# Paired powers on GpSimd, an x ring of fourteen tiles and newly drawn orders in a four-layer graph network

## Chip, cores and metric

The kernel runs on one core of a Trainium2 chip. The metric is the device time in microseconds (us) of one execution. Engines are named as the profile names them: PE (TensorE), DVE (VectorE), ACT (ScalarE), POOL (GpSimd) and SP (SyncE, which issues the loads and stores here).

## What is computed

Thirty-two graphs g, each with 256 nodes of 128 features, pass four pre-norm residual layers. Layers 0 and 3 are graph attention, layer 1 attends with scores of h against itself, and layer 2 is a relational convolution with a bias.

```python
h = jnp.maximum(_layernorm(x, axis=-1), 0.0)
x = x + _L0_gnn_ref(h, adj, L0_gnn_W, L0_gnn_a)
h = jnp.maximum(_layernorm(x, axis=-1), 0.0)
x = x + _L1_gnn_ref(h, adj, L1_gnn_a0, L1_gnn_a1, L1_gnn_a2, L1_gnn_a3)
h = jnp.maximum(_layernorm(x, axis=-1), 0.0)
x = x + _L2_gnn_ref(h, L2_gnn_adj, adj, L2_gnn_weight, L2_gnn_bias)
h = jnp.maximum(_layernorm(x, axis=-1), 0.0)
x = x + _L3_gnn_ref(h, adj, L3_gnn_W, L3_gnn_a)      # _L3 ends in elu
...
def _layernorm(x, axis=-1, eps=1e-05):
    return (x - m) / jnp.sqrt(v + eps)
```

## The kernel before

A unit is one layer of one graph. `ORDER` lists all 128 units: layer 0 of graphs 0 to 15, then layers 1, 2 and 3 of the same sixteen, and then the same four stages for graphs 16 to 31. So there are two halves of four stages of sixteen units. Unit n is number n of this list: 48 to 63 are the first layer 3, 64 to 79 the second layer 0.

Each engine has one instruction stream, built by `pipeline`. It takes a list of (stage function, lag, layers). At step s it calls each stage of the list, in the list's order, for unit s - lag, if that unit's layer is in layers. So the lag says how many steps a stage runs behind the newest unit, and the list's order says what comes first inside a step. Engines meet only at semaphores: a stage waits until the count of the unit that it needs is reached, and everything behind it on its engine waits too.

What a unit passes through, with its lag before:

- DVE `statistics` (0) and `mean_and_variance` (1) give mean and variance of each node (tile mv, two values per partition).
- POOL `inverse_deviation` (0) raises the variance to the power -1/2: one tensor_tensor with pow per unit, on 128x2 values (rs<-mv, L356).
- In layers 0, 1 and 3, POOL `subtract_mean` (0) and `scale_deviation` (1) make h from x: L365, then L373 in place. In layer 2 the DVE's `minus_mean` and the ACT's `normalize` do it, and POOL `add_bias` (2, xb<-x, L384) adds the bias to x in a ring of eight tiles. For the last eight graphs of a half it waits until `residual` (DVE, L708) of the unit eight before has freed its tile.
- PE `put_hT` (3) transposes h (L863), then come `put_edgesT`, `put_v` (L905), `put_z` (L929 in layer 2, 4 or 5 or 6 by layer) and `put_o` (8; L972 in layer 2, L984 and L987 in layers 0 and 3). ACT takes the products out of PSUM, and masks the edges (`mask_edges`, L493, layer 0).
- DVE `residual` (10) writes the new x. In layer 3 ACT's `elu_parts` (9), DVE's `elu` (12) and `add_x` (13, odd graphs) or POOL's `add_x_even` (10, even graphs, L394) make the result.

h has a ring of twelve tiles, and `put_hT` is given only one PSUM bank (bank 0). The x of layer 0 lies in a ring of `XS` = 12 tiles: the first twelve are loaded at the start, and `load_x` on SP reloads a tile after `residual` of layer 0 has read it. SP's list is load_x (lag 10), load_edges (10) and store (11), so in the turn between the halves a load can stand behind a store in SP's stream.

Of the kernel before, what the change touches and what calls it, by code (L numbers as in the profile page):

```python
# [88 lines left out]
def gat_stack(nc, x, adj, w0, a0, m0, m1, m2, m3, w2, b2, w3, a3, out):  # L89
# [10 lines left out]
    with ctx:  # L100
# [233 lines left out]
        def _(pool):  # L334
# [61 lines left out]
            pipeline([(add_x_even, 10, LAST), (inverse_deviation, 0, MULTI_REL), (add_bias, 2, RGCN_REL),  # L396
                      (inverse_deviation, 0, LAST), (scale_deviation, 1, LAST),
                      (scale_deviation, 1, FIRST), (inverse_deviation, 0, RGCN_REL),
                      (scale_deviation, 1, MULTI_REL), (inverse_deviation, 0, FIRST),
                      (subtract_mean, 0, FIRST), (subtract_mean, 0, LAST), (subtract_mean, 0, MULTI_REL)])  # L400
# [3 lines left out]
            with pool.If(pool.value_load(flag[0:1, 0:1], min_val=0, max_val=P) > 0):  # L404
                with pool.Fori(0, B) as g:
                    for layer in range(4):
# [5 lines left out]
                        pool.tensor_tensor(grs[:, :], gve[:, :], minus_half[:, :], ALU.pow).then_inc(g_step, 1)  # L412

        @block.scalar
        def _(act):
# [143 lines left out]
            pipeline([(scale_v, 6, LAST), (take_hT, 4, LAST), (normalize, 5, RGCN_REL),  # L559
                      (mask_edges, 5, FIRST), (scale_hT, 5, MULTI_REL), (take_edgesT, 6, FIRST),  # L560
                      (exponentials_of_s, 5, FIRST), (upper_part, 6, MULTI_REL), (scale_v, 6, FIRST),
                      (exponentials, 7, MULTI_REL), (take_hT, 4, MULTI_REL), (take_hT, 4, FIRST),
                      (exponentials_of_s, 5, LAST), (take_pT, 8, MULTI_REL), (take_mh, 6, RGCN_REL),
                      (elu_parts, 9, LAST)])
# [525 lines left out]
```

## Time and profile before

| what | value |
|---|---|
| median of 3 runs | 291.73 us (291.55 to 292.25) |
| profiled execution | 291.89 us |
| its span, first to last instruction | 290.1 us |
| PE busy | 275.5 us, 95% |
| ACT busy | 259.7 us, 90% |
| DVE busy | 251.4 us, 87% |
| POOL busy | 235.6 us, 81% |
| mean granted TensorE clock | 0.995 |

The profiled execution spends 1.8 us outside of its span. A share of busy time is an average over eight stages with different limits, so what an engine's time is worth has to be read stage by stage. The chain of work that ended last lies 63% on PE, 10% on POOL, 9% on DVE and 8% on ACT.

### The profile page before, as it was taken

The numbers are of one execution on the slowest core, as the hardware profiler recorded it, in microseconds if no ns is written. First come the engines' busy times: TensorE is split into PE (matmuls) and PEld (weight loads), VectorE is DVE, ScalarE is ACT, GpSimd is POOL, SyncE is SP. The second block draws the span as 40 slices with busy tenths as digits, with TensorE's granted clock in tenths as the row PEclk, the third lists the DMA queues.
The fourth block names the chain that finished last, engine by engine and source line by source line (L and its number), as shares of the span: only waits on it lengthen the run. The fifth ranks groups of instructions, "written<-read, shape, count | busy, mean of one in ns | idle before, by whom it ended". The sixth has DMA issues, their size and how long they took to land.

```text
span 290.1 us, 8093 instructions
## 1 busy us (share of the span) xinstructions
PE 275.5 (95%) x2250; PEld 257.0 (89%) x2250; DVE 251.4 (87%) x1217; ACT 259.7 (90%) x850; POOL 235.6 (81%) x376
## 2 busy tenths in 40 slices
PE   2899999999999999999998999999999999999992
PEld 1799998898899999999978899988899999999991
DVE  4788999988888888999988899988878988799985
ACT  4799998999997888898999899899999788889984
POOL 4799876886658999999999988786765799999922
PEclk9999999999999999999999999999999999999998
DMA  5935555500000000011111470000000000001123
GB/s 183 340 105 164 166 166 163 163 5 0 2 1 2 0 2 3 2 54 58 54 49 47 163 239 2 3 0 2 1 2 1 1 2 0 2 5 55 57 71 113
DMA packets 15949, 17.77 MB, mean 61 GB/s; under 512 B 2720, under 2 KB 11808, under 8 KB 15904
## 3 DMA queue, kind: packets, MB, share of 16 engines
q1 hardware_dynamic: 15488, 17.18, 18.6%
q8 instruction: 19, 0.31, 0.4%
q14 instruction: 26, 0.21, 0.2%
q10 hardware_dynamic: 416, 0.07, 0.1%
HBM read 13.05 MB, written 4.19 MB: 59 GB/s over the span
## 4 chain that ended last, share of the span: by engine, by line
PE 63%; POOL 10%; DVE 9%; ACT 8%; issue 7%; DMA 1%; SPq 0%; DVEq 0%; POOLq 0%; ACTq 0%
PE bank L987 20%; PE bank L934 10%; PE bank L929 6%; PE bank L905 5%; PE bank L863 5%; PE bank L954 5%; POOL h L365 3%; DVE pT L688 3%; PE bank L984 3%; PE bank L972 3%; POOL rs L356 3%; PE bank L942 2%; PE bank L936 2%; POOL h L373 2%; ACT relu_y L556 2%
## 5 line engine op out<-in xcount | busy, mean ns | idle before, releaser
L356 POOL TENSOR_TENSOR rs<-mv,minus_half 128x2 f32<-128x2 f32 x128 | 91.5, 715 | 37.8 <-DVE mv L624 36.3
L987 PE MATMUL bank<-val,pT 128*128 128x129 f32 x512 | 74.6, 275 | 0.0
L987 PEld LDWEIGHTS bank<-val,pT 128*128 128x128 f32 x512 | 67.8, 193 | 0.0
L688 DVE SCALAR_TENSOR_TENSOR pT<-bank,val,edgesT 128x256 f32<-128x256 f32 x128 | 55.6, 476 | 5.9 <-ACT edgesT L503 3.1
L373 POOL TENSOR_TENSOR h<-h,rs 128x256 f32<-128x256 f32 x93 | 57.8, 621 | 1.8
L613 DVE BATCH_NORM_STATS2 st<-x 128x6 f32<-128x128 f32 x192 | 45.6, 279 | 0.0
L905 PE MATMUL bank<-w_gat,hT 128*128 128x131 f32 x256 | 41.0, 284 | 2.8 <-ACT hT L484 2.8
L516 ACT ACTIVATE val<-bank,val 128x128 f32<-128x128 f32 x128 | 41.8, 397 | 0.1
L365 POOL TENSOR_TENSOR h<-x,mv 128x256 f32<-128x256 f32 x64 | 41.3, 645 | 0.2
L863 PE MATMUL bank<-ident,h 128*128 128x128 f32 x192 | 38.0, 280 | 1.0 <-POOL h L373 0.7
L905 PEld LDWEIGHTS bank<-w_gat,hT 128*128 128x128 f32 x256 | 34.4, 194 | 4.8 <-ACT val L516 3.5
L624 DVE BATCH_NORM_AGGREGATE mv<-st 128x2 f32<-128x9 f32 x256 | 32.9, 171 | 5.0 <-DVE st L613 0.5
L934 PE MATMUL bank<-hT,haT 128*128 128x256 f32 x128 | 36.7, 382 | 0.0
L984 PE MATMUL bank<-ident,vsum 128*128 128x128 f32 x128 | 35.5, 277 | 0.6 <-DVE x L714 0.3
L987 PEld LDWEIGHTS bank<-h,pT 128*128 128x128 f32 x256 | 31.3, 191 | 2.9
L987 PE MATMUL bank<-h,pT 128*128 128x129 f32 x256 | 33.8, 275 | 0.0
L929 PE MATMUL bank<-edgesT,h 128*128 128x256 f32 x128 | 32.9, 380 | 0.0
L484 ACT ACTIVATE hT<-bank 128x256 f32<-128x256 f32 x64 | 26.9, 421 | 3.5 <-PE bank L863 3.1
L539 ACT ACTIVATE prob<-neg_s,neg_max 128x256 f32<-128x256 f32 x64 | 29.2, 512 | 0.4 <-DVE neg_max L672 0.4
L463 ACT ACTIVATE h<-x,nb,rs 128x128 f32<-128x128 f32 x64 | 27.9, 486 | 0.0
L555 ACT ACTIVATE expy<-bank,rinv 128x128 f32<-128x128 f32 x64 | 25.2, 398 | 2.5 <-DVE rinv L700 2.3
L863 PEld LDWEIGHTS bank<-ident,h 128*128 128x128 f32 x192 | 24.9, 151 | 1.9 <-issue 1.0
(85 smaller groups left out, 651.5 us busy)
## 6 DMA issues: line engine op xcount, KB each, us to landing
edges<-in_adj SPq DMA_DIRECT2D x32, 256.0 KB, 3.3
xin<-in_x SPq DMA_DIRECT2D x32, 128.0 KB, 2.4
out_x<-result SPq DMA_DIRECT2D x32, 128.0 KB, 1.7
w_rel<-in_L_gnn_weight SPq DMA_DIRECT2D x1, 256.0 KB, 3.2
w_gat<-in_L_gnn_W ACTq DMA_DIRECT2D x1, 64.0 KB, 2.7
w_gat<-in_L_gnn_W SPq DMA_DIRECT2D x1, 64.0 KB, 3.2
a_rel<-in_L_gnn_a SPq DMA_DIRECT2D x4, 0.5 KB, 3.8
bias<-in_L_gnn_bias SPq DMA_DIRECT2D x1, 64.0 KB, 3.4
```

Source lines behind the costliest of these rows:

```text
L356: pool.tensor_tensor(rs[:, g % WIDE], mv[:, g % WIDE, :, 1], minus_half[:, :], ALU.pow).then_inc(rs_ready, 1)
L365: pool.tensor_tensor(h[:, n % HS, :, 0:D], xin[:, g % XS] if layer == 0 else x1[:, g % WIDE], mv[:, g % WIDE, :, 0:1].to_broadcast([P, T, ...
L373: pool.tensor_tensor(h[:, n % HS, :, 0:D], h[:, n % HS, :, 0:D], rs[:, g % WIDE, :].rearrange("p (t o) -> p t o", o=1).to_broadcast([P, T, ...
L516: last = act.activation(val[:, k, t, 0:D], bank_v(n)[:, t, 0:D], ACT.Copy, scale=val[:, k, t, D:D + 1])
L613: last = dve.bn_stats(st[:, g % WIDE, t, 0:6], src[:, t])
L688: last = dve.scalar_tensor_tensor(pT[:, n % 4, u], bank_z(n)[:, 0], val[:, k, u, D + 2:D + 3], edgesT[:, g % WIDE, u], ALU.max, ALU.mult)
L863: last = pe.transpose(bank_x(n)[:, t * P:(t + 1) * P], h[:, n % HS, t, 0:D], ident[:, :])
L905: last = pe.matmul(bank_v(n)[:, t], hT[:, n % 4, t * P:(t + 1) * P], w_gat[layer // 3][:, 0:D + 3], start=True, stop=True)
L929: last = pe.matmul(z[:, 0], h[:, n % HS, u, 0:D], edgesT[:, g % WIDE, u], start=(u == 0), stop=(u == T - 1))
L934: pe.matmul(z[:, t], haT[:, n % 4, t * P:(t + 1) * P], hT[:, n % 4], start=True, stop=False, skip_group_check=True)
L984: pe.matmul(bank_o(n)[:, t, 0:D], vsum[:, k:k + 1].to_broadcast([P, P]), ident[:, :], start=True, stop=False, is_transpose=True, skip_grou ...
L987: last = pe.matmul(bank_o(n)[:, t], pT[:, n % 4, u, t * P:(t + 1) * P], values[:, u], start=(u == 0 and layer == 1), stop=(u == T - 1), sk ...
```

## The change

Three things change. First, POOL's power instruction: units 0 to 3 keep one each, and from unit 4 on the odd unit of each pair does both in one instruction on 128x4 values, so the even unit waits for the odd one's variance. The tile of exponents is widened for that. Second, the x ring has fourteen tiles instead of twelve, so two more loads are issued at the start and the second half has two fewer to wait for a freed tile. Third, the lists of all engines are redrawn: most lags outside of POOL grow by one together. Relative to the others, `put_z` of layer 2 (6 to 5), `mask_edges`, `take_edgesT`, `normalize`, `scale_hT`, `upper_part` and `take_mh` (unchanged) come one or two steps earlier; on POOL `subtract_mean` goes from lag 0 to 2 and `scale_deviation` from 1 to 2, `add_bias` from 2 to 0.

```diff
+PAIRED = 4
-XS = 12
+XS = 14
-LAG_MAX = 13
-SP_LAG = 10
+LAG_MAX = 14
+SP_LAG = 11
...
-        minus_half = sb("minus_half", [P, T])
+        minus_half = sb("minus_half", [P, 2, T])
...
-                if ORDER[n] == (1, 0):
+                if ORDER[n] == (1, 1):
...
                 pool.wait_ge(mv_ready, nth(ALL, n))
-                pool.tensor_tensor(rs[:, g % WIDE], mv[:, g % WIDE, :, 1], minus_half[:, :], ALU.pow).then_inc(rs_ready, 1)
+                if n < PAIRED:
+                    pool.tensor_tensor(rs[:, (g % WIDE)], mv[:, (g % WIDE), :, 1], minus_half[:, 0], ALU.pow).then_inc(rs_ready, 1)
+                elif n % 2 == 1:
+                    i = (g % WIDE) - 1
+                    pool.tensor_tensor(rs[:, i:i + 2], mv[:, i:i + 2, :, 1], minus_half[:, :, :], ALU.pow).then_inc(rs_ready, 2)
...
-            pipeline([(add_x_even, 10, LAST), (inverse_deviation, 0, MULTI_REL), (add_bias, 2, RGCN_REL),
...
+            pipeline([(subtract_mean, 2, LAST), (add_x_even, 12, LAST), (subtract_mean, 2, MULTI_REL),
...
-                      (minus_mean, 2, RGCN_REL),
+                      (minus_mean, 5, RGCN_REL),
```

POOL's stream at the turn from layer 2 to layer 3, before. xb is the bias added to x, rs the power, L365 the subtraction of unit 48 and L373 its scaling; the last xb is that of unit 47.

```order
L384 TENSOR_TENSOR xb<-x,bias_less 128x256
L356 TENSOR_TENSOR rs<-mv,minus_half 128x2
L365 TENSOR_TENSOR h<-x,mv 128x2x128
L384 TENSOR_TENSOR xb<-x,bias_less 128x256
L356 TENSOR_TENSOR rs<-mv,minus_half 128x2
L373 TENSOR_TENSOR h<-h,rs 128x2x128
L365 TENSOR_TENSOR h<-x,mv 128x2x128
L356 TENSOR_TENSOR rs<-mv,minus_half 128x2
L373 TENSOR_TENSOR h<-h,rs 128x2x128
```

The same place after the change (line numbers are six or so higher; L361 is the paired power, L370 the subtraction, L378 the scaling).

```order
L361 TENSOR_TENSOR rs<-mv,minus_half 128x4
L389 TENSOR_TENSOR xb<-x,bias_less 128x256
L361 TENSOR_TENSOR rs<-mv,minus_half 128x4
L370 TENSOR_TENSOR h<-x,mv 128x2x128
L378 TENSOR_TENSOR h<-h,rs 128x2x128
L370 TENSOR_TENSOR h<-x,mv 128x2x128
L361 TENSOR_TENSOR rs<-mv,minus_half 128x4
L378 TENSOR_TENSOR h<-h,rs 128x2x128
L370 TENSOR_TENSOR h<-x,mv 128x2x128
```

What moved: before, the power and the subtraction of unit 48 stood ahead of the last xb. Now both stand behind it, and in an odd unit the next pair's power stands between subtraction and scaling.

PE's stream at the same place, before: L929 is `put_z` and L972 `put_o` of layer 2, L863 the transposes of units 48, 49 and 50, L905 `put_v` of unit 48.

```order
L929 MATMUL bank2<-edgesT,h 128x256 x2
L972 MATMUL bank6<-w_rel,mhT 128x128 x2
L929 MATMUL bank3<-edgesT,h 128x256 x2
L972 MATMUL bank7<-w_rel,mhT 128x128 x2
L863 MATMUL bank0<-ident,h 128x128 x2
L929 MATMUL bank2<-edgesT,h 128x256 x2
L972 MATMUL bank6<-w_rel,mhT 128x128 x2
L863 MATMUL bank0<-ident,h 128x128 x2
L905 MATMUL bank5<-w_gat3,hT 128x131 x2
L929 MATMUL bank3<-edgesT,h 128x256 x2
L972 MATMUL bank7<-w_rel,mhT 128x128 x2
L863 MATMUL bank0<-ident,h 128x128 x2
```

And after the change (L935, L978, L869 and L911 are the same four).

```order
L935 MATMUL bank2<-edgesT,h 128x256 x2
L978 MATMUL bank7<-w_rel,mhT 128x128 x2
L935 MATMUL bank3<-edgesT,h 128x256 x2
L978 MATMUL bank6<-w_rel,mhT 128x128 x2
L935 MATMUL bank2<-edgesT,h 128x256 x2
L978 MATMUL bank7<-w_rel,mhT 128x128 x2
L869 MATMUL bank0<-ident,h 128x128 x2
L935 MATMUL bank3<-edgesT,h 128x256 x2
L978 MATMUL bank6<-w_rel,mhT 128x128 x2
L869 MATMUL bank0<-ident,h 128x128 x2
L911 MATMUL bank5<-w_gat3,hT 128x131 x2
L978 MATMUL bank7<-w_rel,mhT 128x128 x2
```

What moved: two z blocks followed the first transpose before, and one does now. The other has gone to the turn from layer 1 to layer 2, so unit 50's transpose comes closer behind unit 49's.

## Rows read from the trace of the kernel before

**Rows 1.** The page of the profile: span and busy time of each engine.
```profile
span 290.1 us, 8093 instructions
PE 275.5 (95%) x2250; PEld 257.0 (89%) x2250; DVE 251.4 (87%) x1217; ACT 259.7 (90%) x850; POOL 235.6 (81%) x376
```

**Rows 2.** Windows inside the layer-1 stage and the turn from layer 3 to layer 0.
```profile
core 0: us, PE busy (x) PEld busy (x) DVE busy (x) ACT busy (x) POOL busy (x), PEclk, DMA share, GB/s
60.00:80.00 20.00, 20.00 (x152) 17.70 (x151) 16.45 (x96) 19.57 (x48) 14.06 (x24) 1.00 0.00 1
142.00:158.00 16.00, 14.55 (x129) 12.74 (x128) 13.57 (x57) 16.00 (x61) 15.29 (x23) 1.00 0.12 43
```

**Rows 3.** Timeline of TensorE, both layer-3 stages; what ended a wait is in brackets.
```profile
130.85 0.38 PE L863 MATMUL bank<-ident,h 128*128 128x128 f32 x2
133.50 0.41 PE L863 MATMUL bank<-ident,h 128*128 128x128 f32 x2 [0.32 <-POOL h L373]
...
265.32 0.38 PE L863 MATMUL bank<-ident,h 128*128 128x128 f32 x2
267.49 0.38 PE L863 MATMUL bank<-ident,h 128*128 128x128 f32 x2
269.49 0.38 PE L863 MATMUL bank<-ident,h 128*128 128x128 f32 x2
272.16 0.41 PE L863 MATMUL bank<-ident,h 128*128 128x128 f32 x2 [0.33 <-POOL h L373]
```

**Rows 4.** Timeline of GpSimd in the second layer-3 stage.
```profile
265.01 0.90 POOL L394 TENSOR_TENSOR result<-expy,x 128x256 f32<-128x256 f32 x1
269.84 0.90 POOL L394 TENSOR_TENSOR result<-expy,x 128x256 f32<-128x256 f32 x1
```

**Rows 5.** Groups by line and form: GpSimd (columns: busy us, mean ns, idle before).
```profile
L356 POOL TENSOR_TENSOR rs<-mv,minus_half 128x2 f32<-128x2 f32 x128 | 91.5, 715 | 37.8 <-DVE mv L624 36.3 <-PE bank L987 1.1
L341 POOL MEMSET minus_half<- 128x2 f32 x1 | 0.1, 100 | 0.0
```

**Rows 6.** Timeline of the turn from layer 2 to layer 3, second half.
```profile
241.08 0.73 POOL L384 TENSOR_TENSOR xb<-x,bias_less 128x256 f32<-128x256 f32 x1
241.75 0.41 DVE L708 TENSOR_TENSOR x<-bank,xb 128x256 f32<-128x256 f32 x1
241.76 0.70 POOL L356 TENSOR_TENSOR rs<-mv,minus_half 128x2 f32<-128x2 f32 x1
...
246.48 0.38 PE L863 MATMUL bank<-ident,h 128*128 128x128 f32 x2
...
248.01 0.38 PE L863 MATMUL bank<-ident,h 128*128 128x128 f32 x2
249.98 0.38 PE L863 MATMUL bank<-ident,h 128*128 128x128 f32 x2
251.49 0.38 PE L863 MATMUL bank<-ident,h 128*128 128x128 f32 x2
```

**Rows 7.** Timeline of GpSimd at the start: subtract, then its dependent multiply.
```profile
10.00 0.62 POOL L365 TENSOR_TENSOR h<-xin,mv 128x256 f32<-128x256 f32 x1
10.69 0.61 POOL L373 TENSOR_TENSOR h<-h,rs 128x256 f32<-128x256 f32 x1
```

**Rows 8.** Chain that ended last, layer 2: one z block of PE (start, us).
```profile
102.76 0.87 PE bank L929 x4
```

**Rows 9.** Timeline around the late x tile of the second layer-0 stage.
```profile
163.87 0.43 SPq L303 DMA_DIRECT2D xin<-in_x  x1
164.77 0.38 PE L863 MATMUL bank<-ident,h 128*128 128x128 f32 x2
166.10 0.49 DVE L613 BATCH_NORM_STATS2 st<-xin 128x6 f32<-128x128 f32 x2 [0.48 <-DMA xin<-in_x]
167.15 0.68 ACT L493 ACTIVATE absent<-edges 128x512 bf16<-128x512 uint32 x1 [1.11 <-DMA edges<-in_adj]
167.70 0.41 PE L863 MATMUL bank<-ident,h 128*128 128x128 f32 x2
```

More of the change, by code:

```diff
@@ L340, in _ @@
                                    pattern=[[-1, P]], channel_multiplier=1).then_inc(ident_ready, 1)
-            pool.memset(minus_half[:, :], -0.5).then_inc(ident_ready, 1)
+            pool.memset(minus_half[:, :, :], -0.5).then_inc(ident_ready, 1)
             pool.memset(ones[:, :], 1.0).then_inc(ident_ready, 1)
@@ L394, in add_x_even @@
                     pool.tensor_tensor(result[:, k], expy[:, n % 4], x1[:, g % WIDE], ALU.add).then_inc(result_ready[0], 1)
-            pipeline([(add_x_even, 10, LAST), (inverse_deviation, 0, MULTI_REL), (add_bias, 2, RGCN_REL),
[L397 to L400, printed above, removed]
+            pipeline([(subtract_mean, 2, LAST), (add_x_even, 12, LAST), (subtract_mean, 2, MULTI_REL),
+                      (scale_deviation, 2, MULTI_REL), (inverse_deviation, 0, LAST),
+                      (inverse_deviation, 0, MULTI_REL), (scale_deviation, 2, LAST),
+                      (inverse_deviation, 0, RGCN_REL), (add_bias, 0, RGCN_REL), (subtract_mean, 2, FIRST),
+                      (scale_deviation, 2, FIRST), (inverse_deviation, 0, FIRST)])
             pool.wait_ge(flag_ready, 1)
@@ L557, in elu_parts @@
                 last.then_inc(y_ready, 1)
[L559 to L564, printed above, removed]
+            pipeline([(scale_v, 7, LAST), (take_hT, 5, FIRST), (take_hT, 5, MULTI_REL),
+                      (exponentials, 8, MULTI_REL), (take_hT, 5, LAST), (take_pT, 9, MULTI_REL),
+                      (normalize, 5, RGCN_REL), (exponentials_of_s, 6, LAST),
+                      (exponentials_of_s, 6, FIRST), (scale_hT, 5, MULTI_REL), (upper_part, 6, MULTI_REL),
+                      (scale_v, 7, FIRST), (elu_parts, 10, LAST), (take_mh, 6, RGCN_REL),
+                      (mask_edges, 5, FIRST), (take_edgesT, 6, FIRST)])
             act.wait_ge(flag_ready, 1)
@@ L731, in add_x @@
                     dve.tensor_tensor(result[:, k], expy[:, n % 4], x1[:, g % WIDE], ALU.add).then_inc(result_ready[1], 1)
-            pipeline([(invert_sums, 10, LAST), (mean_and_variance, 1, RGCN_REL), (elu, 12, LAST),
-                      (invert_sums, 10, FIRST), (mean_and_variance, 1, LAST), (take_rows, 7, FIRST),
-                      (take_z, 7, MULTI_REL), (statistics, 0, MULTI_REL), (minus_mean, 2, RGCN_REL),
-                      (residual, 10, RGCN_REL), (residual, 10, FIRST), (mean_and_variance, 1, FIRST),
-                      (add_x, 13, LAST), (center_early, 2, FIRST), (statistics, 0, RGCN_REL),
-                      (mean_and_variance, 1, MULTI_REL), (invert_sums, 10, MULTI_REL),
-                      (statistics, 0, LAST), (take_rows, 7, LAST), (rectify, 3, MULTI_REL),
-                      (statistics, 0, FIRST), (residual, 10, MULTI_REL)])
+            pipeline([(statistics, 0, RGCN_REL), (invert_sums, 11, LAST), (invert_sums, 11, FIRST),
+                      (elu, 13, LAST), (statistics, 0, MULTI_REL), (add_x, 14, LAST),
+                      (residual, 11, FIRST), (take_z, 8, MULTI_REL), (mean_and_variance, 1, LAST),
+                      (minus_mean, 5, RGCN_REL), (residual, 11, RGCN_REL),
+                      (mean_and_variance, 1, RGCN_REL), (statistics, 0, LAST),
+                      (invert_sums, 11, MULTI_REL), (take_rows, 8, FIRST),
+                      (mean_and_variance, 1, MULTI_REL), (rectify, 4, MULTI_REL), (take_rows, 8, LAST),
+                      (mean_and_variance, 1, FIRST), (residual, 11, MULTI_REL), (center_early, 2, FIRST),
+                      (statistics, 0, FIRST)])
             dve.wait_ge(scores_taken, COUNTS[MULTI_REL][-1])
```

10 lines of the change are left out of this document (5 added, 5 removed).

## Prediction

> **What bounds the kernel now.** I read the page first. PE is busy 275.5 of 290.1 us, and no other engine is over 90% [rows 1]. Then I read windows by stage. In 60 to 80 us, the layer-1 stage, PE is busy 20.00 of 20 while POOL has 14.06 [rows 2]. Nothing that POOL saves there can show, and the same holds wherever PE's transposes follow each other at their even pace. So I looked on PE's timeline for transposes that come late, and for what ended the wait.
>
> There are three such places. In layer 3 PE runs a pair of units in 4.17 us (265.32 to 269.49), in steps of 2.17 and 2.00. Late in each layer-3 stage one step is 2.65 or 2.67 instead of 2.17, and the bracket says that the transpose waited for POOL's scaling of h [rows 3]. That is 0.5 us in each half. The reason is on POOL's timeline: with its share of the final additions POOL needs 4.83 us for a pair (265.01 to 269.84) [rows 4], against PE's 4.17. It starts the stage ahead and loses 0.66 per pair until its lead is gone.
>
> The second place is the turn from layer 3 to layer 0. In 142 to 158 us ACT is busy 16.00 of 16, POOL 15.29, and PE only 14.55 [rows 2]. ACT is the bound there. The redrawn lists give ACT the same instructions there: `mask_edges` keeps its lag while the others grow by one, but it now stands behind `elu_parts` in the list instead of ahead of it, so the number of masks done before the last `elu_parts` stays at four. I expect no change from that.
>
> The third is 164 to 168 us. A reload of x is issued at 163.87, the statistics that need it begin at 166.10 after a wait of 0.48, and ACT's mask waits 1.11 for edges until 167.15. PE's step there is 2.93 long (164.77 to 167.70) [rows 9].
>
> **The powers.** Before, 128 powers take 91.5 us, 0.715 each [rows 5]. After, 4 single and 62 paired ones remain. What a power on 128x4 costs, p, no row shows. The lower bound is no cost for the added elements: p = 0.70. The upper bound takes all as per element except what a memset of the same 128x2 values takes, 0.10 [rows 5]: 0.10 + 2 x 0.6 = 1.30. Moving elements is cheap: a subtraction of 256 of them takes 0.62 [rows 7], less than the power of two. So the question is only whether the arithmetic of the power repeats per element. I take 0.85, nearer to the bottom, since the same two-operand form moves 254 more elements in less time; both ends stay in the range. At 0.85, POOL saves 62 x (1.43 - 0.85) = 36 us of work, nearly all of it where POOL waits for others anyhow: before the powers alone it idled 37.8 us [rows 5].
>
> The Trainium skill speaks against the change. GPSIMD Engine Reference, section 2.1, puts the dispatch of an instruction at "tens of cycles", and section 1 gives each core 16 lanes for its 16 partitions, so that the elements of a partition come one after another. By that page nearly all of 0.7 us would be work per element, and p would be near the top end. This hangs on the rows only by their upper bound; no run here has shown it.
>
> **Layer 3.** POOL's pair of 4.83 us holds two powers, each 0.69 or 0.70 long and, if spaced as xb is (0.73 long, the next begins 0.68 later [rows 6]), 0.64 apart. After: 4.83 - 1.28 + (p - 0.05) = 3.5 + p, 4.35 us at 0.85. That loses 0.18 per pair instead of 0.66, so the lead lasts and both waits of 0.5 go: **-1.0 us**. In the first half ACT is close behind, so its half of this is less sure. I keep it.
>
> **The turn from layer 2 to layer 3.** This is where the new order can cost. The last xb (unit 47) waits for `residual` of unit 39, and before, power and subtraction of unit 48 stood ahead of it; now they stand behind it. Queued behind the wait are thus all of layer 3's h, and PE's transposes wait for those. The row of that residual is 241.75, 0.41 long, so it ends at 242.16, and PE wants h of unit 48 at 246.48 [rows 6]. Between o of unit 39 and this transpose PE has four blocks of z and o in either order, so the distance holds. After: 242.16 + 0.68 (xb) + p + 0.69 (subtraction and its wait) + 0.61 (scaling) [rows 6, 7] = 244.14 + p. The lead is 2.34 - p. Unit 49: PE comes 1.53 later (248.01), POOL 0.56 + p + 0.56 later, as the pair's power now stands between; lead 2.75 - 2p. Unit 50: PE's step was 1.97, but the z block of 0.87 in it [rows 8] has gone elsewhere, so 1.10; POOL 1.25; lead 2.60 - 2p. Unit 51: PE 1.51, POOL 1.12 + p; lead 3.0 - 3p. At 0.85 this is +0.4: **0 us**. It turns negative at p = 1.0, or at 0.9 with 0.1 per hand-over for semaphores. The z block itself costs nothing, it only runs earlier, under a PE that is full there.
>
> **The x ring.** Tiles 28 and 29 now come in the first half; only 30 and 31 wait for a freed tile, two steps later relative to their use. The wait of 0.48 goes [rows 9]. The edges behind it in SP's stream are still issued after the store, so the wait of 1.11 stays, though scaling and exponentials now stand ahead of the mask. I take **-0.5 us**; at best it is 1.0, if half of the mask's wait goes with it [rows 9]. The two more loads at the start are issued ahead of the weights of layers 1 and 2, which nothing needs during layer 0: 0.
>
> **The rest of the orders.** In layer 2 `minus_mean` has three more steps to wait for rs, which covers the even unit's wait for its partner. Units 0 to 3 stay single, so the start isn't held up. Transposes before z and v inside a step give the same instructions per step. 0 us, by the cover of PE's own work; without it, a wait of some 0.1 to 0.5 per half.
>
> **Sum.** -1.0 - 0.5 = -1.5 against the profiled 291.89 us (span 290.1 and 1.8 around it) gives 290.4; the median of the runs is 0.16 lower, so **290.2 us**.
>
> **Rivals.**
> A, the forecast, p up to about 0.95: chance 0.52, 290.2 us, own range 288.9 to 291.2. The lower end has all of the edge wait's step back as well and some 0.5 at the start from the transposes' earlier place.
> B, p between 0.95 and 1.1: small stalls of 0.1 to 0.4 in each half at the turn to layer 3, layer 3's waits still shortened; 290.9 us, chance 0.13.
> C, the other side, p above 1.1, the arithmetic repeats per element. At 1.3 the lead of unit 51 is -0.9: PE stalls that long in each half, +1.8. POOL then has 4.8 per pair in layer 3 as before, but starts without a lead, so that the wait of 0.5 grows, up to 0.9 more per half. With -0.5 for x: 1.3 to 3.1 slower, 293.8 us. Against it stands only the cheap 254 elements, for it that the power is the longest of POOL's small operations. Chance 0.25. It decides from p = 1.0 on. The page named above would give this case.
> D, the change brings nothing: POOL's relief is taken up by ACT and DVE, which are at 90% and 87% [rows 1], and the next wait in layer 3 takes the old one's place. 291.6 us, chance 0.10.
>
> **How the numbers follow.** The measurement tells some 0.3%, 0.9 us, from no change. A puts 0.43 on faster, 0.07 on same, 0.02 on slower; B 0.06, 0.05, 0.02; C 0.00, 0.05, 0.20; D 0.01, 0.07, 0.02. Together 0.50, 0.24, 0.26. The range runs from A's low end to a little above C's middle, 288.9 to 294.2, and leaves out less than 2 in 10.
>
> **What would show it.** The mean of the 128x4 power is the first row to read: under 0.95 or not. Right if POOL's idle time grows, if no transpose in the two layer-3 stages waits for POOL's scaling, if steps of PE at the turn to layer 3 are unbroken, and if only the start still waits for x. Wrong if transposes of units 48 to 53 wait for POOL, if PE's busy share in the turn between the halves falls below 14.55 of 16, or if the new in-step orders open waits on PE inside the layer-0 stages, where I count none.

## The result, and the profile after

The changed kernel takes 293.03 us of device time (median of 7 runs, 292.63 to 294.58), against 291.73 us for the kernel before on the same chip (7 runs). The ratio is 1.0048, with a 95% interval from 1.0037 to 1.0059: slower, where 290.2 us and faster was forecast. The profiled execution took 293.03 us. On the page of the changed kernel PE's busy time is hardly less than in [rows 1], POOL's has fallen by 19 us, and DVE's has risen:

```profile
span 291.2 us, 8119 instructions
...
PE 274.9 (94%) x2250; PEld 257.7 (88%) x2250; DVE 256.4 (88%) x1217; ACT 258.9 (89%) x850; POOL 216.4 (74%) x314
```

Next the groups by line and shape of the changed kernel: the paired power, PE's transposes, POOL's xb addition, DVE's `minus_mean` (nb) and the four single powers. After the bar stand busy us and mean ns, then the idle time ahead of them and what ended it.

```profile
L361 POOL TENSOR_TENSOR rs<-mv,minus_half 128x4 f32<-128x4 f32 x62 | 64.6, 1041 | 30.2 <-DVE mv L629 29.2 <-PE bank L993 1.0
...
L869 PE MATMUL bank<-ident,h 128*128 128x128 f32 x192 | 38.0, 281 | 3.4 <-POOL h L378 1.9 <-DVE h L636 1.4
...
L389 POOL TENSOR_TENSOR xb<-x,bias_less 128x256 f32<-128x256 f32 x32 | 23.3, 729 | 16.9 <-DVE mv L629 15.9 <-DVE x L713 1.0
...
L648 DVE SCALAR_TENSOR_TENSOR nb<-mv,rs 128x2 f32<-128x2 f32 x32 | 10.7, 335 | 0.9 <-POOL rs L361 0.5
...
L358 POOL TENSOR_TENSOR rs<-mv,minus_half 128x2 f32<-128x2 f32 x4 | 2.8, 698 | 4.1 <-DVE mv L629 4.1
```

The first and last lines give the missing price: p is 1.04 us, the single power 0.70. PE's transposes wait 1.9 us for POOL's scaling (five times, over the whole span). And `minus_mean`, the same work as before, has grown. Its group in the kernel before, for comparison:

```profile
L643 DVE SCALAR_TENSOR_TENSOR nb<-mv,rs 128x2 f32<-128x2 f32 x32 | 6.6, 207 | 0.0
```

**Where the time went.** In both timelines of PE I took the start of every unit's transpose and subtracted; call the difference PE's lateness. Layer 2 (units 32 to 47 and 96 to 111) has no such transpose, so the stretches from 31 to 52 and from 94 to 116 hold all of it. The table gives how that difference grows over each stretch of units, after minus before, in us; a second column does the same for experiment e4_xb_16 (below).

| stretch (units) | forecast | after | e4_xb_16 |
|---|---|---|---|
| start to the end of layer 1 (to 31) | 0 | -0.14 | +0.95 |
| turn from layer 2 to 3 (31 to 52) | 0 | +1.95 | 0.00 |
| layer 3 (52 to 63) | -0.5 | -0.52 | -0.52 |
| turn from layer 3 to 0, to layer 1 (63 to 94) | -0.5 | -1.21 | -2.28 |
| second turn from layer 2 to 3 (94 to 116) | 0 | +1.65 | +0.01 |
| second layer 3 (116 to 127) | -0.5 | -0.62 | -0.62 |
| sum | -1.5 | +1.11 | -2.46 |

The sum +1.11 is the difference of the spans, 291.2 to 290.1. So gains came at the three places where they were counted, and the turn from layer 2 to 3 took them back, in both halves. The small first row hides two parts that cancel: PE's transposes are 0.73 earlier at unit 6, and lose 0.85 again between units 16 and 18, at the turn to layer 1 (-0.93 to -0.08). No run was made on those.

**The turn from layer 2 to 3.** PE's transposes of units 112 to 115, second half, changed kernel; before, they began at 246.48, 248.01, 249.98 and 251.49 [rows 6]:

```profile
247.63 0.41 PE L869 MATMUL bank<-ident,h 128*128 128x128 f32 x2
249.75 0.41 PE L869 MATMUL bank<-ident,h 128*128 128x128 f32 x2 [0.40 <-POOL h L378]
251.07 0.41 PE L869 MATMUL bank<-ident,h 128*128 128x128 f32 x2
253.19 0.41 PE L869 MATMUL bank<-ident,h 128*128 128x128 f32 x2 [0.42 <-POOL h L378]
```

They wait for POOL. It begins with one long stop. The addition xb of unit 104 is the first of its half that needs a tile freed by a residual, that of unit 96. POOL's row of it and DVE's row of that residual, changed kernel, and below the dots the same addition in the kernel before:

```profile
233.89 0.73 POOL L389 TENSOR_TENSOR xb<-x,bias_less 128x256 f32<-128x256 f32 x1 [4.38 <-DVE mv L629]
233.29 0.42 DVE L713 TENSOR_TENSOR x<-bank,xb 128x256 f32<-128x256 f32 x1
...
232.91 0.72 POOL L384 TENSOR_TENSOR xb<-x,bias_less 128x256 f32<-128x256 f32 x1 [0.18 <-DVE x L708]
```

The first bracket names the variance (mv), but the variance of unit 104 was ready at 229.71; the residual ended at 233.71 and POOL went on 0.18 later. So this stop of 4.38 us is the ring wait, and so are the stops of 0.52 and 0.53 before the even units that follow. Together they are 5.9 us in each half, against 0.2 before. POOL's timeline at the end of layer 2, same kernel (start, length, in brackets a wait and what ended it):

```profile
240.42 1.02 POOL L361 TENSOR_TENSOR rs<-mv,minus_half 128x4 f32<-128x4 f32 x1
241.41 0.73 POOL L389 TENSOR_TENSOR xb<-x,bias_less 128x256 f32<-128x256 f32 x1
242.66 0.72 POOL L389 TENSOR_TENSOR xb<-x,bias_less 128x256 f32<-128x256 f32 x1 [0.52 <-DVE x L713]
243.34 1.02 POOL L361 TENSOR_TENSOR rs<-mv,minus_half 128x4 f32<-128x4 f32 x1
244.33 0.73 POOL L389 TENSOR_TENSOR xb<-x,bias_less 128x256 f32<-128x256 f32 x1
245.02 1.02 POOL L361 TENSOR_TENSOR rs<-mv,minus_half 128x4 f32<-128x4 f32 x1
246.11 0.62 POOL L370 TENSOR_TENSOR h<-x,mv 128x256 f32<-128x256 f32 x1
246.88 0.61 POOL L378 TENSOR_TENSOR h<-h,rs 128x256 f32<-128x256 f32 x1
```

DVE's timeline in the same microseconds, `minus_mean` (L648) and `residual` (L713) alone, other instructions between them left out:

```profile
241.47 0.68 DVE L648 SCALAR_TENSOR_TENSOR nb<-mv,rs 128x2 f32<-128x2 f32 x1 [0.26 <-POOL rs L361]
242.08 0.41 DVE L713 TENSOR_TENSOR x<-bank,xb 128x256 f32<-128x256 f32 x1
...
244.46 0.62 DVE L648 SCALAR_TENSOR_TENSOR nb<-mv,rs 128x2 f32<-128x2 f32 x1
245.00 0.41 DVE L713 TENSOR_TENSOR x<-bank,xb 128x256 f32<-128x256 f32 x1
...
246.13 0.12 DVE L648 SCALAR_TENSOR_TENSOR nb<-mv,rs 128x2 f32<-128x2 f32 x1
```

Read them together; they close a loop. The xb at 242.66 waited for the residual of 242.08, eight units back in its ring. The paired power comes behind it in POOL's list at 243.34 and ends at 244.36. DVE's `minus_mean` of 244.46 needs the deviation that this power made. It started under the next xb (244.33) and lasts until that xb ends, 245.06, though the same instruction takes 0.12 at 246.13, with no addition of the bias under way. Behind it in DVE's list stands the residual of 245.00, for which the next xb of an even unit would wait. From residual to residual the loop takes 2.92 us for two units, and POOL's powers come at that pace (237.50, 240.42, 243.34). PE's products of layer 2 come 2.62 apart per pair; of one unit and of the second behind it:

```profile
240.43 0.61 PE L978 MATMUL bank<-w_rel,mhT 128*128 128x128 f32 x4
...
243.05 0.61 PE L978 MATMUL bank<-w_rel,mhT 128*128 128x128 f32 x4
```

So after the long stop POOL falls another 0.3 behind PE with each pair while PE sees nothing of it, and the first h of layer 3 comes late. Whether this loop is the cause is what the experiments had to show. **Theory 1** in them is the wait for the ring of eight xb tiles and the loop that it makes. **Theory 2** is that a paired power of 1.04 us is by itself too long for layer 3's front. **Theory 3** is that `put_z` of layer 2, moved from lag 6 to 5, took away PE work that used to cover POOL.

**The turn from layer 3 to 0.** It gains 1.21 in all, but it has a hole of its own. TensorE's transposes of units 65 and 66 with the transposes of edges between them, changed kernel:

```profile
143.17 0.38 PE L869 MATMUL bank<-ident,h 128*128 128x128 f32 x2
...
145.34 0.38 PE L895 MATMUL bank<-ident_bf,absent 128*128 128x128 bf16 x4 [1.12 <-ACT absent L498]
...
146.71 0.38 PE L869 MATMUL bank<-ident,h 128*128 128x128 f32 x2
```

That step is 3.54, against 2.80 before. In the window of 142 to 158 us, whose columns are those of [rows 2], PE has 13.54 of 16 and ACT 15.46, no longer all:

```profile
142.00:158.00 16.00, 13.54 (x128) 12.80 (x127) 14.52 (x61) 15.46 (x63) 15.26 (x22) 1.00 0.17 59
```

### The profile page after: what moved, and what is told of

It reads as the page before. It is cut to its first block, busy times and chain, and to the rows that moved or that the text cites. A ratio compares the mean times of both kernels' runs of the same rounds, so it can differ in the third digit from the quotient of the medians.

```text
span 291.2 us, 8119 instructions
## 1 busy us (share of the span) xinstructions
PE 274.9 (94%) x2250; PEld 257.7 (88%) x2250; DVE 256.4 (88%) x1217; ACT 258.9 (89%) x850; POOL 216.4 (74%) x314
## 4 chain that ended last, share of the span: by engine, by line
PE 68%; DVE 13%; ACT 6%; issue 5%; POOL 5%; DMA 1%; SPq 0%; DVEq 0%; ACTq 0%; POOLq 0%
PE bank L993 24%; PE bank L940 10%; PE bank L911 7%; PE bank L869 6%; PE bank L960 5%; PE bank L990 4%; PE bank L948 4%; DVE st L618 3%; DVE pT L693 3%; PE bank L942 2%; PE bank L935 2%; PE bank L895 2%; POOL rs L361 2%; DVE mv L629 2%; DVE x L713 2%
## 5 line engine op out<-in xcount | busy, mean ns | idle before, releaser
L361 POOL TENSOR_TENSOR rs<-mv,minus_half 128x4 f32<-128x4 f32 x62 | 64.6, 1041 | 30.2 <-DVE mv L629 29.2
L378 POOL TENSOR_TENSOR h<-h,rs 128x256 f32<-128x256 f32 x93 | 57.5, 618 | 6.7 <-POOL h L370 0.4
L618 DVE BATCH_NORM_STATS2 st<-x 128x6 f32<-128x128 f32 x192 | 44.8, 275 | 0.0
L521 ACT ACTIVATE val<-bank,val 128x128 f32<-128x128 f32 x128 | 42.8, 413 | 0.1
L370 POOL TENSOR_TENSOR h<-x,mv 128x256 f32<-128x256 f32 x64 | 40.1, 627 | 1.7 <-DVE mv L629 0.4
L869 PE MATMUL bank<-ident,h 128*128 128x128 f32 x192 | 38.0, 281 | 3.4 <-POOL h L378 1.9
L911 PE MATMUL bank<-w_gat,hT 128*128 128x131 f32 x256 | 40.6, 282 | 0.0
L389 POOL TENSOR_TENSOR xb<-x,bias_less 128x256 f32<-128x256 f32 x32 | 23.3, 729 | 16.9 <-DVE mv L629 15.9
L911 PEld LDWEIGHTS bank<-w_gat,hT 128*128 128x128 f32 x256 | 34.5, 195 | 0.6 <-ACT val L521 0.5
L489 ACT ACTIVATE hT<-bank 128x256 f32<-128x256 f32 x64 | 27.5, 429 | 7.6 <-PE bank L869 7.5
L677 DVE CUSTOM_DVE_ANT_0 neg_s<-bank,upper 128x256 f32<-128x256 f32 x64 | 24.5, 421 | 10.1 <-ACT upper L539 10.0
L935 PE MATMUL bank<-edgesT,h 128*128 128x256 f32 x128 | 33.0, 381 | 0.0
L869 PEld LDWEIGHTS bank<-ident,h 128*128 128x128 f32 x192 | 22.7, 144 | 7.9 <-issue 3.2
```

Source lines behind the costliest of these rows:

```text
L361: pool.tensor_tensor(rs[:, i:i + 2], mv[:, i:i + 2, :, 1], minus_half[:, :, :], ALU.pow).then_inc(rs_ready, 2)
L370: pool.tensor_tensor(h[:, n % HS, :, 0:D], xin[:, g % XS] if layer == 0 else x1[:, g % WIDE], mv[:, g % WIDE, :, 0:1].to_broadcast([P, T, ...
L378: pool.tensor_tensor(h[:, n % HS, :, 0:D], h[:, n % HS, :, 0:D], rs[:, g % WIDE, :].rearrange("p (t o) -> p t o", o=1).to_broadcast([P, T, ...
L521: last = act.activation(val[:, k, t, 0:D], bank_v(n)[:, t, 0:D], ACT.Copy, scale=val[:, k, t, D:D + 1])
L618: last = dve.bn_stats(st[:, g % WIDE, t, 0:6], src[:, t])
L869: last = pe.transpose(bank_x(n)[:, t * P:(t + 1) * P], h[:, n % HS, t, 0:D], ident[:, :])
```

## The experiments

Twelve kernels ran; each ratio is to the kernel before on the same chip. "Turn" in the text is the turn from layer 2 to 3, and a loss at it is the growth of PE's lateness from unit 31 to 52 and from 94 to 116, as in the table above.

**e4_xb_16: sixteen xb tiles, no ring wait.** The changed kernel, in which xb has its own tile for each graph of a half. Every instruction keeps its place.

```diff
-        xb = sb("xb", [P, SLOTS, T, D])
+        xb = sb("xb", [P, WIDE, T, D])
...
-                if g % WIDE >= SLOTS:
-                    pool.wait_ge(o_taken, nth(NOT_LAST, n - SLOTS))
```

> The changed kernel with sixteen xb tiles instead of eight, so that add_bias never waits for a residual of its half; all orders unchanged. Theory 1: as with the later bias, 289.5 us, since the wait and not the place of the instruction makes the loop. POOL's idle time before xb on the residual goes to 0. If the place matters as well (the DVE's minus_mean held by POOL's additions of the bias), somewhat more than that, 290 to 291. Theories 2 and 3: 293.0.

Measured: 288.42 us (288.22 to 289.44, 4 runs), ratio 0.9882, 95% interval 0.9868 to 0.9897. It is the fastest kernel of the study and beats both. Its losses at the turn are 0.00 and +0.01 (table above). POOL's timeline in the second turn:

```profile
236.03 1.02 POOL L361 TENSOR_TENSOR rs<-mv,minus_half 128x4 f32<-128x4 f32 x1
...
238.65 1.02 POOL L361 TENSOR_TENSOR rs<-mv,minus_half 128x4 f32<-128x4 f32 x1 [0.22 <-DVE mv L627]
...
240.62 1.02 POOL L361 TENSOR_TENSOR rs<-mv,minus_half 128x4 f32<-128x4 f32 x1 [0.25 <-DVE mv L627]
...
242.47 0.61 POOL L378 TENSOR_TENSOR h<-h,rs 128x256 f32<-128x256 f32 x1
```

Its groups, of the transposes and of xb:

```profile
L867 PE MATMUL bank<-ident,h 128*128 128x128 f32 x192 | 38.2, 282 | 2.0 <-DVE h L634 2.0
...
L387 POOL TENSOR_TENSOR xb<-x,bias_less 128x256 f32<-128x256 f32 x32 | 23.2, 729 | 6.8 <-DVE mv L627 6.8
```

The powers of the first two rows are 2.62 apart, PE's own pace, and POOL waits for variances only. The first h is ready at 243.08 and PE takes it at 245.49, so there are 2.4 us of lead; no transpose waits for POOL any more. The powers cost 1.03 here as well, which refutes theory 2 as the cause of this loss. And put_z is where the change put it: as long as POOL isn't late, its moved cover costs nothing (e11_z_6 below has what it is worth when POOL is late).

**e5_before_xb_16: the same edit in the kernel before.** It asks whether the ring wait cost anything there.

```diff
-        xb = sb("xb", [P, SLOTS, T, D])
+        xb = sb("xb", [P, WIDE, T, D])
...
-                if g % WIDE >= SLOTS:
-                    pool.wait_ge(o_taken, nth(NOT_LAST, n - SLOTS))
```

> The kernel before with sixteen xb tiles. In the trace of before, the ring's wait stands 0.4 us before xb in all and no transpose of units 48 to 53 waits. If the ring of eight costs only together with the paired power and the bias at lag 0 (theory 1): within 0.3 us of 291.7. If the longer ring is a gain by itself, whatever the change did: 290.7 or less.

Measured: 291.69 us (291.46 to 292.11, 10 runs), ratio 1.0002, interval 0.9993 to 1.0012. Nothing. Before, `add_bias` ran at lag 2 and `residual` at 10, so that the addition of unit n met the residual of unit n - 8 in the same step. Afterwards the lags are 0 and 11: the addition asks three steps ahead of the residual. The wait is made by the new lags; it was harmless with the old ones.

**e1_bias_later: add_bias at lag 4 instead of 0.** The changed kernel with its ring of eight, in which the addition comes behind the residual that it waits for.

```diff
-                       (inverse_deviation, 0, RGCN_REL), (add_bias, 0, RGCN_REL), (subtract_mean, 2, FIRST),
+                       (inverse_deviation, 0, RGCN_REL), (add_bias, 4, RGCN_REL), (subtract_mean, 2, FIRST),
```

> The changed kernel with add_bias four steps later on POOL, nothing else. Theory 1 (the ring of eight xb tiles makes a loop between POOL and DVE): the bias of a unit no longer waits for the residual of the unit eight before, so the paired power behind it is not held, and POOL is free for layer 3's h at once. The transposes of units 48 to 51 then come without a wait, which took 1.9 and 1.6 us in the two halves: 293.0 - 3.5 = 289.5 us. Theory 2 (the paired power of 1.04 us is by itself too slow for the first units of layer 3): the waits stay, within 0.5 us of 293.0. Theory 3 (the earlier z block of layer 2 takes away cover): also unchanged, 293.0.

Measured: 293.82 us (292.87 to 294.36, 6 runs), ratio 1.0067, interval 1.0051 to 1.0083. Theory 1 wanted 289.5 here and missed. The losses at the turn are +1.86 and +1.59, as large as in the changed kernel. POOL's timeline at the second turn, and PE's transpose of unit 114:

```profile
244.90 0.72 POOL L389 TENSOR_TENSOR xb<-x,bias_less 128x256 f32<-128x256 f32 x1
245.59 0.61 POOL L370 TENSOR_TENSOR h<-x,mv 128x256 f32<-128x256 f32 x1
246.34 0.61 POOL L378 TENSOR_TENSOR h<-h,rs 128x256 f32<-128x256 f32 x1
246.91 0.73 POOL L389 TENSOR_TENSOR xb<-x,bias_less 128x256 f32<-128x256 f32 x1
...
249.72 0.74 POOL L389 TENSOR_TENSOR xb<-x,bias_less 128x256 f32<-128x256 f32 x1
```

```profile
251.93 0.41 PE L869 MATMUL bank<-ident,h 128*128 128x128 f32 x2 [0.71 <-POOL h L378]
```

Ahead of this the xb additions come in pairs of 1.44 with no wait on a residual, so the loop is gone. But the last two additions now stand behind the first h of layer 3 and ahead of the next ones, 0.7 us each, just where POOL has no slack. One wait was traded for work in the wrong place. That is my account of the miss; the next run tests it.

**e7_xb_16_bias_later: both edits.** Sixteen tiles, so no ring wait is left, and add_bias at lag 4.

```diff
-        xb = sb("xb", [P, SLOTS, T, D])
+        xb = sb("xb", [P, WIDE, T, D])
...
-                       (inverse_deviation, 0, RGCN_REL), (add_bias, 0, RGCN_REL), (subtract_mean, 2, FIRST),
+                       (inverse_deviation, 0, RGCN_REL), (add_bias, 4, RGCN_REL), (subtract_mean, 2, FIRST),
```

> Sixteen xb tiles and the bias four steps later. The later bias alone gained nothing. If that was because four additions of the bias (0.68 us each) now fall among layer 3's first units on POOL, this kernel loses most of what sixteen tiles brought: 291.5 to 293.5 us, with waits for POOL's scaling at units 50 and 51. If the later bias was slow for what is left of the ring's wait, this kernel is as fast as with sixteen tiles alone, 288.4.

Measured: 293.89 us (292.93 to 294.07, 4 runs), ratio 1.0078, interval 1.0061 to 1.0095. Losses at the turn are +1.59 and +1.57, without any ring wait. Against e4_xb_16 only the place of the additions differs, and it costs 5.5 us of the median: they are 3.2 at the two turns, 1.1 at the turn from layer 3 to 0 (-1.23 instead of -2.28), and the rest doesn't show between the profiled executions, of which this one was the fastest of its kernel (292.93) and that of e4_xb_16 the slowest (289.44). So e1's miss is explained by the displaced additions, and it says nothing against the ring wait as the cause in the changed kernel.

**e2_single_powers: all 128 powers single, new orders kept.**

```diff
-PAIRED = 4
+PAIRED = 128
```

> The changed kernel with a single power per unit throughout, orders and x ring as changed. Theory 1 with the power's size as a part of it: the loop has xb, one power of 0.70 and the DVE's part for each unit, so it is 2 x 0.34 us shorter in the chain but two powers per pair cost 1.4 instead of 1.04 on POOL; the turn from layer 2 to 3 loses about as much or up to 1 us more per half, and layer 3 waits for POOL's scaling again, 0.5 per half: 294 to 295 us. Theory 2 (the pairing is what costs): it falls back towards 291.0.

Measured: 294.50 us (294.03 to 296.0, 6 runs), ratio 1.0104, interval 1.0086 to 1.0123. Slower than the changed kernel by 1.5: the pairing helps. The losses at the turn are still +1.55 and +1.57. So the ring wait costs nearly as much under single powers. There it is one stop: 3.41 us ahead of the xb at 234.62, and none before the seven that follow, so no loop. But POOL then has a power and an addition for each unit, 1.36 us (242.06 to 243.42) against PE's 1.31, so that what it lost at the stop it can't make up. With pairs, two additions and a power take POOL 2.5 us where it doesn't wait (e4_xb_16: powers at 233.51 and 236.03), so there the loop's 2.92, and not POOL's own work, makes it fall further behind. Pairing adds at most 0.4 to the loss of the first turn. This takes more weight from theory 2.

**e8_xb_16_single: sixteen tiles and single powers.**

```diff
-PAIRED = 4
+PAIRED = 128
...
-        xb = sb("xb", [P, SLOTS, T, D])
+        xb = sb("xb", [P, WIDE, T, D])
```

> Sixteen xb tiles, a single power per unit, orders and x ring as changed: what the pairing is worth when the loop is gone. A pair of powers costs 1.4 us instead of 1.0, which is 0.2 per unit on POOL. By the two waits of 0.5 us in layer 3 that the changed kernel no longer has: 289.4 us. By nothing, if the sixteen tiles give POOL lead enough: 288.4.

Measured: 291.11 us (290.28 to 292.64, 8 runs), ratio 0.9989, interval 0.9967 to 1.0011. No loss at the turns (+0.01 and 0.00). Against e4_xb_16 pairing is worth 2.7 us, and the place is not the one of the forecast alone: over layer 3 (52 to 63) it is +0.08 here and -0.52 there, over the turn from layer 3 to 0 (63 to 94) -0.42 and -2.28, over the second layer 3 -0.60 and -0.62.

**e11_z_6: put_z of layer 2 back to lag 6**, the changed kernel otherwise. Theory 3 by itself.

```diff
-                      (put_hT, 4, FIRST), (put_o, 9, MULTI_REL), (put_z, 5, RGCN_REL), (put_z, 6, FIRST),
+                      (put_hT, 4, FIRST), (put_o, 9, MULTI_REL), (put_z, 6, RGCN_REL), (put_z, 6, FIRST),
```

> The changed kernel (eight xb tiles, paired powers) with put_z of layer 2 at lag 6, so that one z block of 0.87 us lies again between the transposes of units 48 and 51. Theory 3 (the earlier z takes away cover): most of the 1.9 and 1.6 us of waits in the two halves goes, 290 us. Theory 1 (the loop between POOL and DVE makes h late by the ring): the later units gain only what the cover hides, up to 0.9 us per half, and the pairs of powers in layer 2 stay 2.92 us apart: 291.3 to 293.0.

Measured: 299.64 us (298.96 to 300.1, 4 runs), ratio 1.0265, interval 1.0244 to 1.0286. Between units 31 and 52 the loss is 4.64 instead of 1.95. Most of it, 3.56, arises at the turn from layer 1 to 2, by PE's first product of layer 2: `take_mh` on ACT kept its lag of 6, so ACT reaches it before PE has made the product that it takes. One line of its waits list, and ACT's and PE's rows at that turn:

```profile
ACT mhT L526 <- PE bank L935: 16.1, 32, 1.4
```

```profile
94.93 0.38 ACT L526 ACTIVATE mhT<-bank 128x256 f32<-128x256 f32 x1 [1.41 <-PE bank L935]
```

```profile
95.94 1.13 PE L993 MATMUL bank<-h,pT 128*128 128x129 f32 x8 [1.05 <-ACT pT L551]
```

ACT stands 1.41 us in `take_mh`, its `take_pT` comes behind it, and PE waits 1.05 for that. The changed kernel's waits list has 4.9 us in 22 waits for the same line. So the run isn't a clean undoing: for that, take_mh would have had to move as well. But the other turn can be read in it. From the last product of layer 2 that is still in step (unit 43) to unit 52, PE's lateness grows by 1.07 in the first half and 1.01 in the second, where the changed kernel loses 1.95 and 1.65. So the z block, back in its old place, hides 0.9 and 0.6 of POOL's lateness and not the rest, as theory 1 expected, and POOL's additions of even units are still 2.92 apart (243.56, 246.48). Theory 3 is a part of the loss, not its cause: without the ring wait nothing is left for the block to cover.

**e3_ring_12 and e6_before_ring_14: the x ring alone.** The first is the changed kernel with twelve x tiles, the second the kernel before with fourteen.

```diff
-XS = 14
+XS = 12
```

> The changed kernel with an x ring of twelve tiles. The turn between the halves gained 1.2 us with the change. If it was the ring: 293.0 + 0.5 to 1.2 = 293.5 to 294.2 us, and a wait of DVE's statistics for x returns at about 166 us. If it was the new order or the relieved POOL: 293.0 us, with the wait in the trace but covered.

```diff
-XS = 12
+XS = 14
```

> The kernel before with an x ring of fourteen tiles. By my forecast the wait of DVE's statistics for x at 166 us goes and PE's turn is 0.5 us shorter: 291.2. If the ring of fourteen only brings two more loads into the start: 291.7 or up to 0.5 more.

Measured: 294.32 us (293.5 to 295.06, 6 runs), ratio 1.0083, interval 1.0066 to 1.0101; and 291.63 us (291.28 to 292.61, 10 runs), ratio 0.9997, interval 0.9988 to 1.0007. In the new order the larger ring gives back 0.57 between units 63 and 94 (-1.21 with it, -0.64 without); the rest of the 1.3 us between the medians I can't place, since in the profiled execution of the twelve PE was also 1.0 us later by unit 31, an offset that arises in the first units (see the last section). But it isn't the place that I had read. At the step of unit 74, 2.93 before, the new order has 2.29 with twelve tiles, although DVE waits 1.13 for x there, and 2.23 with fourteen; 0.42 of the 0.57 come at the step of unit 82 instead (3.28 against 2.86). In the old order the larger ring gives nothing: the step of unit 74 stays at 2.91, and ACT's mask still waits for edges, 1.75 us. So the wait for x that I counted at 0.5 was not what made that step long.

**e9_xb_16_turn and e12_turn_and_mask: the hole at the turn from layer 3 to 0.** On top of e4_xb_16, first PE's put_edges behind its put_o, then also ACT's masks ahead of elu_parts, as the lists had it before the change. The second goes one unit further than that: with elu_parts at lag 10 the first mask comes behind the elu parts of eleven units, where it was twelve before and in the changed kernel.

```diff
-                      (put_edgesT, 6, FIRST), (put_o, 9, RGCN_REL), (put_o, 9, LAST), (put_hT, 4, LAST),
+                      (put_o, 9, RGCN_REL), (put_o, 9, LAST), (put_edgesT, 6, FIRST), (put_hT, 4, LAST),
```

> Sixteen xb tiles, and on PE put_edgesT of layer 0 moved behind put_o of layer 3 inside a step. In the changed kernel PE waited 1.12 us for ACT's first mask at 145 us with put_o queued behind; in the kernel with sixteen tiles that wait is not seen any more. If ACT sets the turn: no change, 288.4 us. If PE's list order still holds ready work behind the masks: up to 1 us less, 287.5.

```diff
-                      (scale_v, 7, FIRST), (elu_parts, 10, LAST), (take_mh, 6, RGCN_REL),
-                      (mask_edges, 5, FIRST), (take_edgesT, 6, FIRST)])
+                      (scale_v, 7, FIRST), (mask_edges, 5, FIRST), (elu_parts, 10, LAST), (take_mh, 6, RGCN_REL),
+                      (take_edgesT, 6, FIRST)])
```

> As the run with the moved put_edgesT, and ACT's mask_edges ahead of elu_parts in its list. The mask comes 1.0 us earlier in each of five steps, the last masks are one more before ACT's last elu_parts. If ACT sets the turn, one more mask in it costs 0.5 us: 289.0. If masks were what PE waits for: 287.5.

Measured: 288.68 us (288.13 to 289.45, 4 runs), ratio 0.9893, interval 0.9869 to 0.9918; and 289.62 us (288.44 to 290.09, 4 runs), ratio 0.9914, interval 0.9889 to 0.9940. Neither can be told from e4_xb_16. The step of unit 66 does fall, from 2.46 to 2.23 in both, but the steps of 69 and 70 rise from 2.40 and 2.73 to 3.04 and 3.10, and over 63 to 94 the three kernels have -2.28, -2.22 and -2.22. ACT is busy 16.00 of 16 us from 142 to 158 in all three, and these orders only choose in which step its shortage shows.

**e10_power_widths: the disputed price by itself.** The kernel before with 24 more POOL instructions at its start, each twice: powers on 1, 2, 4, 8, 16, 32, 64 and 128 columns, and subtractions on 2, 4, 8 and 128. The operands are columns of the identity matrix. The whole kernel starts later by them, so its time says nothing.

```diff
+            for op, widths in ((ALU.pow, (1, 2, 4, 8, 16, 32, 64, 128)), (ALU.subtract, (2, 4, 8, 128))):
+                for width in widths:
+                    for _ in range(2):
+                        pool.tensor_tensor(prob_flat[:, at:at + width], ident[:, 0:width], ident[:, 0:width],
+                                           op).then_inc(probed, 1)
```

> The kernel before with 24 more instructions on POOL at the start: powers on 1, 2, 4, 8, 16, 32, 64 and 128 columns and subtractions on 2, 4, 8 and 128, each twice. Two columns took 0.70 and four 1.04 us in the kernels. If a power costs a fixed part and 0.17 per column: 0.53, 0.70, 1.04, 1.7, 3.1, 5.8, 11, 22 us. If it works in groups of columns, the durations are steps. The time of the whole is about 50 us longer for it and says nothing.

Measured: one run, 378.14 us. The groups by shape (a shape with both operations has one mean for both):

```profile
L353 POOL TENSOR_TENSOR prob<-ident 128x64 f32<-128x64 f32 x2 | 21.0, 10519 | 0.0
L353 POOL TENSOR_TENSOR prob<-ident 128x32 f32<-128x32 f32 x2 | 10.8, 5414 | 0.0
L353 POOL TENSOR_TENSOR prob<-ident 128x16 f32<-128x16 f32 x2 | 5.8, 2893 | 0.0
...
L353 POOL TENSOR_TENSOR prob<-ident 128x4 f32<-128x4 f32 x4 | 2.3, 604 | 0.0
L353 POOL TENSOR_TENSOR prob<-ident 128x2 f32<-128x2 f32 x4 | 1.7, 444 | 0.0
L353 POOL TENSOR_TENSOR prob<-ident 128x1 f32<-128x1 f32 x2 | 1.1, 562 | 0.1
```

From 32 to 64 columns it is (10519 - 5414) / 32 = 160 ns per column, from 16 to 32 it is 158, and 5414 - 32 x 160 leaves 0.3 us fixed. A power on 128x1 costs 0.56. With the kernel's own 0.70 for two columns and 1.04 for four, it is about 0.3 to 0.4 us fixed and 0.16 or 0.17 per column.

## Why the prediction was wrong, step by step

**The price of the power** was the open question of the forecast, and it was not what decided. I took 0.85 by the likeness to a subtraction, and p is 1.04. The arithmetic repeats per column, and the fixed part is larger than the 0.10 of my upper bound; the truth lies between the ends. So the powers' own time fell by 24 us (91.5 to 64.6 + 2.8), not by 36. The estimate by the Trainium skill, GPSIMD Engine Reference, sections 1 and 2.1, would have been near 1.3. It is right that the elements of a partition come one after another, by the rows of e10_power_widths. Its dispatch of "tens of cycles", an estimate of less than 0.1 us by the 1.2 GHz clock that section 1 gives GpSimd, does not cover the 0.3 to 0.4 us that those rows leave.

**The turn from layer 2 to 3, 0 us, is the step that failed**: it measured +1.95 and +1.65. The mis-sized p is the small part. Put 1.04 into the lead of unit 51, 3.0 - 3p, and it comes to -0.1 us, where 0.85 gave +0.4. The large part is the start of the sum. I let the last xb follow its residual at 242.16 and took that residual as a fixed time, set by PE. But POOL's add_bias had moved three steps ahead of the residual it waits for, so POOL ran into the ring wait in the last eight graphs, at 233.89 and again as at 242.66. Between the xb of an even unit and that of the odd one behind it stands a paired power of the same list, which I didn't count. And the residual itself waited behind a `minus_mean` that needs that power and stood until POOL's xb was over. In the trace of after the whole chain begins later: the scaling of the first h starts at 246.88, ready at 247.49, where my sum has 244.14 + 1.04 = 245.18. PE itself stands 0.94 later there (its product of unit 103 begins at 241.74, before at 240.80), which costs no lead; the other 1.37 us are lead that is gone. Taken from the lead of unit 51 they give -1.5, and the loss of that half is 1.65. So the rest of the sum was right, and its start was not. With the ring wait taken away the sum's 0 holds, at the measured p: e4_xb_16 loses 0.00 and 0.01. That removal, with all orders and the pairing kept, shows that the ring wait is what costs the 1.9 and 1.6. That the wait works as a loop with DVE is read from the timeline, 2.92 against 2.62 per pair. No run took away DVE's part alone, so how the loss divides between the long stop, the paired power and the held `minus_mean` stays open. e2_single_powers shows 1.55 of the first turn's 1.95 without the pairing and without the loop.

**Layer 3, -1.0**, was right in size: -0.52 and -0.62. For the first half so is the cause, since without the pairing the gain is not there (+0.08 in e8_xb_16_single). In the second half that kernel gains 0.60 with single powers, so there the new order alone is enough. The steps that waited before are 2.17 now. POOL's time per pair was to be 3.5 + p, so 4.54; two stretches of the changed kernel's POOL timeline, from scaling to scaling, give 269.27 - 264.95 = 4.32 and 273.86 - 269.27 = 4.59:

```profile
264.95 0.60 POOL L378 TENSOR_TENSOR h<-h,rs 128x256 f32<-128x256 f32 x1
...
269.27 0.61 POOL L378 TENSOR_TENSOR h<-h,rs 128x256 f32<-128x256 f32 x1
...
273.86 0.88 POOL L378 TENSOR_TENSOR h<-h,rs 128x256 f32<-128x256 f32 x1
```

**The x ring, -0.5**: the wait went, and the larger ring is worth 0.57 in the new order, mostly at another step than mine (e3_ring_12); alone it is worth nothing (e6_before_ring_14). That the size fits is luck. The mask's wait of 1.11 for edges, which I let stand, is gone too: the waits list of the changed kernel has none.

**The orders at the turn from layer 3 to 0, no change**, was wrong in both directions. The count of masks was right, but I had not looked at who asks for them: PE now has put_edgesT ahead of put_o in a step and so wants the first mask one block of put_o earlier. The elu parts ahead of that mask are those of the same unit as before, but they waited 0.54 for DVE, and the mask is done at 145.19, before at 144.19. Together this makes the step of 3.54. Against that the steps of units 65, 69 and 70 are shorter by 0.54, 0.57 and 0.45 than before. I had counted none of these. The e4 kernel gains 1.1 more here with the same lists, and all of it is this one step, 2.46. With single powers and no ring wait (e8_xb_16_single) the step is 3.58 again, and with the displaced additions (e7_xb_16_bias_later) 3.53. So the hole comes with whatever makes POOL late before it; that this reaches ACT by way of DVE is likely, but was not tried by itself.

**The rivals.** None of the four is what happened. C had the right sign and the right place, by a condition (p above 1.1) that did not hold. B had the right p and stalls four times too small. So 293.03 us lies in the stated range by luck: the range reached that far for the sake of C. Two of the signs named for being wrong did come, the transposes that wait for POOL and the 13.54 of 16 in the turn between the halves. A ring wait that the new lags open was no rival of mine, though the two lags, 0 against 11, stood in the diff.

## What to carry to other kernels

When a stage moves to an earlier lag, look up every wait on a freed tile in it and compare its distance in steps with the stage that frees the tile: here 2 against 10 was free and 0 against 11 cost 3.6 us at two turns, while eight more tiles took that back and made the change a gain of 1.2%. Don't take the name in a wait's bracket for the cause without a look at when that one was done. A chain that starts at "the other engine is done at this time" is only as good as the check that the other engine doesn't wait for this one; if it does, count all instructions once round, of both engines. Moving work later to escape a wait is not free either: the same additions four steps later cost what the wait had.

## What the hardware showed that I had not expected

A power on GpSimd costs 0.56 us for one column of 128 partitions and 0.16 us more per column (10.52 at 64); a subtraction of 256 columns is done in 0.62. For powers, joining two instructions saves only the fixed part: 2 x 0.70 becomes 1.04.

A tiny DVE instruction with both inputs in SBUF (`minus_mean` on 128x2) takes 0.12 us alone and 0.62 or 0.68 when it starts early under POOL's xb addition; its end falls 0.02 behind that of POOL's. It starts under an addition and is held 16 times out of 32 in both kernels, but before it came late in the addition and took at most 0.30. By the mean it went from 207 to 335 ns. The Trainium skill says this (SBUF — State Buffer, section "SBUF: two separate sides": the shared port pair is "an exclusive lock, not a bandwidth split", and a DVE instruction with two SBUF inputs blocks on a GpSimd instruction that reads SBUF and started first), and for the additions this trace agrees, with these numbers; I had not brought it to bear on the order. For the power it doesn't: in e4_xb_16 four `minus_mean` started 0.14 us into a paired power of 1.02 and took 0.13 or 0.14.

The start of the kernel differs by over 1 us between profiled executions whose code there is the same: at unit 31 the changed kernel stands at -0.14, e4_xb_16 at +0.95 and e12_turn_and_mask at +1.51. The difference is there by unit 5, where DVE waits for the first loads of x (one wait of 1.38 at 8.48 in e4_xb_16 that the changed kernel doesn't have). So a single span tells stages apart only after that offset is taken out.
